# First attention of a Flamingo-style block on one core: the subtraction of the row maximum folded into the exp

## The reference

```
q = latents @ Wq                                   # 8 heads of 64
kv = concat([x, latents]) @ Wkv ; k, v = split(kv)
q = l2norm(q) * q_scale ; k = l2norm(k) * k_scale
sim = einsum('bhid,bhjd->bhij', q, k) * 8.0
sim = where(mask, sim, -max)
attn = softmax(sim)
out = layer_norm(einsum('bhij,bhjd->bhid', attn, v) @ Wo)
x = x + tanh(g) * out
```

## Time and profile before

| | us |
|---|---|
| median of 3 runs | 398.12 (397.4 to 398.33) |
| the profiled execution | 397.01 |
| its span in the trace | 394.9 |
| first attention, about | 24 to 192 of the span |
| experts, about | 192 to 260 |
| second attention and last part | 260 to 395 |

### The profile page before, as it was taken

How to read it: one execution, slowest core, us unless ns; L and a number is a source line. 1 busy time by engine, 2 the same in 40 slices (tenths; PEclk the granted TensorE clock), 3 DMA queues, 4 the chain that set the end, 5 groups by cost and what they waited for, 6 DMA issues and landing times. The chain is left out here.

```text
span 394.9 us, 10468 instructions
## 1 busy us (share of the span) xinstructions
PE 367.7 (93%) x3588; PEld 272.4 (69%) x3601; DVE 321.5 (81%) x916; ACT 262.1 (66%) x528; POOL 219.5 (56%) x380
## 2 busy tenths in 40 slices
PE   7799989999999999999999999999979999986785
PEld 6356656666676676667766788878867888765664
DVE  2989999899998998988746588756458899999796
ACT  2377767777777777776765222245658999887885
POOL 4655559666666667762604000007685887788653
PEclk9899999999999999999999999999999999999589
DMA  5989999900000000000000000000000000000003
GB/s 166 259 151 123 121 135 118 108 1 2 2 2 2 2 1 2 2 2 2 3 1 2 0 2 0 2 1 2 0 2 2 3 4 2 2 4 2 0 16 93
DMA packets 61034, 13.26 MB, mean 34 GB/s; under 512 B 51108, under 2 KB 60344, under 8 KB 60984
## 3 DMA queue, kind: packets, MB, share of 16 engines
q1 hardware_dynamic: 60196, 12.37, 22.9%
q10 hardware_dynamic: 660, 0.23, 0.2%
q0 software_dynamic: 128, 0.00, 0.0%
HBM read 11.55 MB, written 1.05 MB: 32 GB/s over the span
## 5 line engine op out<-in xcount | busy, mean ns | idle before, releaser
L407 POOL TENSOR_TENSOR a_rn<-a_ssq,neghalf 128x8 f32<-128x8 f32 x48 | 79.0, 1653 | 24.4 <-DVE a_ssq L1019 19.8
L90 POOL TENSOR_TENSOR nrow<-mrow 128x2 f32<-128x2 f32 x32 | 6.3, 196 | 56.8 <-DVE mrow L86 56.5
L1019 DVE TENSOR_REDUCE a_ssq<-q_home 128x8 f32<-128x512 f32 x48 | 32.2, 672 | 6.4 <-ACT q_home L798 6.2
L501 PE MATMUL a_x<-wkv_a,a_kvT 128*128 128x512 f32 x64 | 35.5, 637 | 1.2 <-ACT a_kvT L791 1.0
L804 ACT ACTIVATE kv_home<-a_x,maskcol 128x512 f32<-128x512 f32 x32 | 21.9, 684 | 19.9 <-PE a_x L501 19.9
L423 POOL TENSOR_TENSOR a_yr<-a_ymv,eps_row 128x1 f32<-128x1 f32 x16 | 3.0, 189 | 37.8 <-DVE a_ymv L1062 37.8
L1038 DVE TENSOR_REDUCE a_mx<-a_s 128x4 f32<-128x512 f32 x32 | 21.9, 686 | 2.0 <-PE a_s L527 1.9
L1950 DVE TENSOR_REDUCE b_mx<-b_s 128x16 f32<-128x1024 f32 x16 | 19.5, 1218 | 4.3 <-PE b_s L1548 4.0
L515 PEld LDWEIGHTS a_m<-ident,q_home 128*128 128x128 f32 x128 | 15.8, 143 | 9.7 <-issue 9.0
L816 ACT ACTIVATE kv_home<-a_m,cols 128x512 f32<-128x512 f32 x32 | 21.9, 685 | 0.6 <-PE a_m L515 0.4
L546 PE MATMUL a_m<-kv_home,p_home 128*64 128x65 f32 x512 | 22.0, 228 | 0.3 <-ACT p_home L826 0.3
(11 more groups left out here) (301 smaller groups left out, 1144.6 us busy)
## 6 DMA issues: line engine op xcount, KB each, us to landing
w_gu<-in_L_ffn_Wg_dram SPq DMA_DIRECT2D x4, 512.0 KB, 9.7
w_gu<-in_L_ffn_Wu_dram SPq DMA_DIRECT2D x4, 512.0 KB, 11.9
w_d<-in_L_ffn_Wd_dram SPq DMA_DIRECT2D x8, 256.0 KB, 8.0
out_dram<-xs SPq DMA_DIRECT2D x8, 128.0 KB, 1.8
xs<-in_x_dram SPq DMA_DIRECT2D x1, 640.0 KB, 7.6
cs<-in_ctx_dram SPq DMA_DIRECT2D x1, 640.0 KB, 9.1
wkv_a<-in_L_xattn_Wkv_dram SPq DMA_DIRECT2D x2, 256.0 KB, 6.6
nat<-in_L_ffn_w_dram SPq DMA_DIRECT2D x2, 256.0 KB, 3.2
```

What stands on the lines that cost most here:

```text
L407: nc.gpsimd.tensor_tensor(rn[:, tp, i, :], ssq[:, tp, i, :], neghalf[:, 0:H0], ALU.pow)\
L501: nc.tensor.matmul(p_x[:], kvT[:, tp, b * 2 * S:(b + 1) * 2 * S], wkv_a[:, INNER:2 * INNER], start=True, stop=True).then_inc(vproj_done, 1)
L1019: nc.vector.tensor_reduce(ssq[:, tp, i, :], sq[:, i, :].rearrange("p (h d) -> p h d", h=H0), AX.X, ALU.add).then_inc(reduced, 1)
```

## The change

The keys' scale becomes -8 instead of 8, so the banks hold negated scores. VectorE reduces each bank with a minimum (`row_least`, into `mn`), which is the negated maximum. ScalarE computes exp(-1 * negated score + mn), head by head, straight from the bank: four ACTIVATEs of 128 columns with `mn`'s column as bias, since a bias is one value per row and each head has its own. The subtraction and its semaphores `maxed` and `shifted` are gone. TensorE's `scores(t)` waits for the exps of tile t-1 (`exped`), and the first shared gate too. `row_least(s-2, 1)` stands where `shift(s-2, 0)` stood in VectorE's list.

```diff
--- before.py
+++ after.py
@@ -247,7 +247,7 @@
         kvT = sb("kvT", [P, 2, 4 * S])
         ssq = sb("ssq", [P, 2, 3, H0])
         rn = sb("rn", [P, 2, 3, H0])
-        mx = sb("mx", [P, 2, HP])
+        mn = sb("mn", [P, 2, HP])
         rsum = sb("rsum", [P, 2, HP])
         yst = sb("yst", [P, 2, 6])
         ymv = sb("ymv", [P, 2, 2])
@@ -280,9 +280,9 @@
         norms_ready, xn_ready, xT_done, affined, kv_masked, proj_done, squared, reduced, normed, scaled = (
             sem(n) for n in ("norms_ready", "xn_ready", "xT_done", "affined", "kv_masked", "proj_done", "squared",
                              "reduced", "normed", "scaled"))
-        vproj_done, v_ready, weigh_ready, q_turned, k_turned, qT_ready, kT_ready, scored, maxed, shifted, exped = (
+        vproj_done, v_ready, weigh_ready, q_turned, k_turned, qT_ready, kT_ready, scored, least_ready, exped = (
             sem(n) for n in ("vproj_done", "v_ready", "weigh_ready", "q_turned", "k_turned", "qT_ready", "kT_ready",
-                             "scored", "maxed", "shifted", "exped"))
+                             "scored", "least_ready", "exped"))
         pT_done, prT_ready, mixed, inverted, att_ready, attT_done, attT_ready = (
             sem(n) for n in ("pT_done", "prT_ready", "mixed", "inverted", "att_ready", "attT_done", "attT_ready"))
         y_done, y_stats, y_rstd, y_read, xb_ready, x_new, root_ready = (
@@ -520,7 +520,7 @@
                 pe.wait_ge(kT_ready, 2 * t + 2)
                 if t == 0:
                     pe.wait_ge(maskcol_ready, 1)
-                wait(pe, shifted, 2 * t)
+                wait(pe, exped, 2 * t)
                 for h in range(HP):
                     for a, b in ((0, 0), (1, 1), (0, 1), (1, 0)):
                         half = slice(a * DH0, (a + 1) * DH0)
@@ -601,7 +601,7 @@
 
             def shared_gate(i):
                 if i == 0:
-                    pe.wait_ge(shifted, 2 * NT)
+                    pe.wait_ge(exped, 2 * NT)
                 if i == 1:
                     pe.wait_ge(weights_out, 3)
                     pe.wait_ge(xrT_ready, 2)
@@ -817,8 +817,13 @@
                                      scale=cols[:, 4:5]).then_inc(kT_ready, 1)
 
             def exp(t, a):
-                act.wait_ge(shifted, 2 * t + a + 1)
-                nc.scalar.activation(pr[:, a], pr[:, a], ACT.Exp).then_inc(exped, 1)
+
+                act.wait_ge(least_ready, 2 * t + a + 1)
+                wait(act, pT_done, 2 * (t - 1) + a + 1)
+                for h in range(HP):
+                    last = nc.scalar.activation(pr[:, a, h, :], p_s[a][:, h * P:(h + 1) * P], ACT.Exp,
+                                                bias=mn[:, a, h:h + 1], scale=-1.0)
+                last.then_inc(exped, 1)
 
             def probs_out(t, a):
                 act.wait_ge(pT_done, 2 * t + a + 1)
@@ -989,7 +994,7 @@
                     last = nc.vector.tensor_copy(maskcol[b * S:(b + 1) * S, b:B:2], p_s0[b * S:(b + 1) * S, b:B:2])
                 last.then_inc(maskcol_ready, 1)
                 dve.wait_ge(scale_in, 16 * 4)
-                nc.vector.scalar_tensor_tensor(cols[:, 4:5], cols[:, 8:9], 8.0, cols[:, 9:10], ALU.mult, ALU.mult)\
+                nc.vector.scalar_tensor_tensor(cols[:, 4:5], cols[:, 8:9], -8.0, cols[:, 9:10], ALU.mult, ALU.mult)\
                     .then_inc(scale_ready, 1)
 
             def gate_rows():
@@ -1033,17 +1038,11 @@
                                                proj_bank[i][:].rearrange("p (h d) -> p h d", h=H0),
                                                ALU.min, ALU.mult).then_inc(scaled, 1)
 
-            def row_max(t, a):
+            def row_least(t, a):
+
                 dve.wait_ge(scored, t + 1)
-                nc.vector.tensor_reduce(mx[:, a, :], p_s[a][:].rearrange("p (h k) -> p h k", h=HP), AX.X, ALU.max)\
-                    .then_inc(maxed, 1)
-
-            def shift(t, a):
-                s3 = p_s[a][:].rearrange("p (h k) -> p h k", h=HP)
-                dve.wait_ge(maxed, 2 * t + a + 1)
-                wait(dve, pT_done, 2 * (t - 1) + a + 1)
-                nc.vector.tensor_tensor(pr[:, a], s3, mx[:, a, :].unsqueeze(2).to_broadcast([P, HP, P]),
-                                        ALU.subtract).then_inc(shifted, 1)
+                nc.vector.tensor_reduce(mn[:, a, :], p_s[a][:].rearrange("p (h k) -> p h k", h=HP), AX.X, ALU.min)\
+                    .then_inc(least_ready, 1)
 
             def attend(t, a):
                 dve.wait_ge(mixed, 2 * t + a + 1)
@@ -1158,25 +1157,21 @@
                 if exists(s - 1, NT):
                     scale(s - 1, (s - 1) % 2, 0)
                 if exists(s - 2, NT):
-                    row_max(s - 2, 0)
+                    row_least(s - 2, 0)
                 if exists(s - 1, NT):
                     reduce(s - 1, (s - 1) % 2, 2)
                     scale(s - 1, (s - 1) % 2, 1)
                 if exists(s - 2, NT):
-                    shift(s - 2, 0)
+                    row_least(s - 2, 1)
                 if exists(s - 3, NT):
                     attend(s - 3, 0)
                     attend(s - 3, 1)
                 if exists(s, NT):
                     replace_masked(s, s % 2)
-                if exists(s - 2, NT):
-                    row_max(s - 2, 1)
                 if exists(s - 1, NT):
                     scale(s - 1, (s - 1) % 2, 2)
                 if exists(s - 7, NT):
                     next_input(s - 7)
-                if exists(s - 2, NT):
-                    shift(s - 2, 1)
                 if exists(s - 5, NT):
                     row_stats(dve, s - 5, (s - 5) % 2, x_new)
                 if exists(s - 4, NT):
```

## The result

The changed kernel takes **403.46 us** (median of 4 runs, 403.17 to 403.5) against 397.76 for the kernel before beside it (median of 4, 397.07 to 398.33): ratio 1.014, 95% interval 1.0122 to 1.0157, so 4.9 to 6.2 us slower. Its profiled execution took 403.5 us with a span of 401.7, 6.8 more than the span before. The forecast was 405.1 in a range of 402.0 to 409.0.

A forecast was written before the change was run, and what follows sets the result against it. TensorE was taken to bound the steady turn of 10.79 us, with VectorE having slack. Terms 7.8 + 1.1 + 0.5 - 2.4 = +7.0 us on a profiled 397.0 gave 404.0, or 405.1 against the median of 398.1; range 402.0 to 409.0.

The forecast's parts named there:

- The loop: Steady turn: scores, TensorE's list through the keys' projection, Square, exp, scores; each turn 0.56 us longer.
- E: Time from the first exp piece's start to the last one's end in a bank, forecast 1.15 us.
- two-pointer rival: Each exp piece costs what the affine ACTIVATE costs, E 1.52: +12.9, 411.0 us; chance 0.06.
- short pieces: Exp pieces as short as plain copies, E 0.75: +0.6, 398.7 us; chance 0.05.
- tiles 1 to 14: Scores of these tiles each wait for the exp of bank 1: 14 x 0.56 = +7.8 us.
- given back in those turns: TensorE's waits for VectorE in turns 3 to 5 go as the subtractions are dropped: -2.4 us.
- tile 15: Turn without projections, where the exp starts later against the scores: +1.1 us.
- behind it, to the first shared gate: Last exp: tile 15's second-bank transposes and the tail wait for the longer exp, +0.5 us.
- VectorE as hidden pace-setter: Short hidden TensorE waits for VectorE in steady turns vanish: 396.1 us with 0.6 a turn; chance 0.05.
- ScalarE spilling over: Each exp's growth of 0.53 also reaches TensorE another way once per turn: 7.4 more, 412.5 us; chance 0.04.

The follow-up runs named there:

- no maximum: The kernel with both exps early, with the row minimum left out and one exp of 512 per bank: 395.04 us, 0.9943 of the kernel before.
- split-and-wait kernel: Kernel before, with each exp cut into four of 128 in SBUF and the scores waiting for the exps: 408.46 us, 1.0278 of before.
- both exps early: Changed kernel with bank 0's exp moved ahead of the first values on ScalarE and bank 1's right behind them: 394.33 us, 0.9916 of the kernel before.
- the split alone: Kernel before, with each exp of 512 cut into four of 128 in SBUF, the scores still waiting for the subtraction: 398.91 us, 1.0045 of before.
- one exp: Changed kernel with one exp of 512 columns per bank, using the first head's bias for all heads: 399.03 us, 0.9992 of the kernel before.
- changed again: The changed kernel run once more without any edit, on the same chip as its variants: 406.64 us, 1.0224 of the kernel before.

## Why the prediction was right

**The loop.** The step on which it all rested was that the exp starts behind the Square, and the Square behind TensorE's projection, so a turn is a fixed part plus E. Four values of E where the scores wait for the exp give 10.86 at 0.62, 10.92 at 0.68, 11.38 at 1.14 and 11.50 at 1.26: each is E + 10.24. The prediction's fixed part was 11.35 - 1.15 = 10.20. Most of the rest is the release: 0.14 from the exp's end to the scores' start, where 0.11 was taken from the key copy (181.88 to 181.98 in the earlier trace rows is 0.10).

**E.** Forecast 1.15 (pieces of 0.37, 0.26 apart), measured 1.13 to 1.15 with pieces of 0.373. By the Trainium skill's figures (ScalarE: Activation LUTs, What ACT_TABLE_LOAD costs) E was an estimated 1.27; the trace of the changed kernel stays below that, and the pieces out of SBUF, at 0.39 and 1.26 for four, come to the page's figures. The two-pointer rival (1.52) and the short pieces (0.75) both fall.

**The terms.** All from the starts of the scores in the two traces.

| term | forecast | measured |
|---|---|---|
| tiles 1 to 14 | 14 x 0.56 = 7.8 | 14 x 0.59 = 8.3 |
| given back in those turns | -2.4 | 5.26 - 8.3 = -3.0 |
| tile 15 | 1.1 | 9.58 - 8.50 = 1.08 |
| behind it, to the first shared gate | 0.5 | 11.72 - 11.33 = 0.39 |
| sum | 7.0 | 6.73 |

The 5.26 is tile 0's scores to tile 14's, 155.82 us after and 150.56 before. Only this sum is measured in the changed kernel; its split into 8.3 and -3.0 rests on the kernel with no maximum, where neither the new wait nor VectorE's waits are left: there the stretch is 147.61, which is 2.95 under before, and with 14 x 0.59 it comes to 155.87. So both terms were forecast too small, by 0.5 and 0.6, and that the sum is off by only 0.3 is in part luck: the two errors cancel. The rows of after that answer to the earlier trace rows:

```profile
187.19 1.14 ACT L824 ACTIVATE p_home<-a_s,a_mn 128x128 f32<-128x128 f32 x4
...
193.66 1.15 ACT L824 ACTIVATE p_home<-a_s,a_mn 128x128 f32<-128x128 f32 x4
```

```profile
188.47 1.10 PE L527 MATMUL a_s<-kv_home,q_home 64*64 64x128 f32 x32 [1.52 <-ACT p_home L824]
...
194.86 0.66 PE L537 MATMUL a_m<-ident,p_home 128*128 128x128 f32 x4 [0.41 <-ACT p_home L824]
```

**What VectorE gives back.** The waits of the earlier trace rows are gone in the profile after: the turns 4 and 5, 11.06 and 12.78 before, are 11.38 like the rest. The prediction named two reasons, a VectorE with less to do and a TensorE that arrives later. The runs show that they do not add. The split-and-wait kernel, which keeps the subtractions, pays 7.9 where 14 x 0.71 = 9.9 would stand (158.45 from tile 0's scores to tile 14's), so it gets 2 of the 3 us back by its late TensorE alone. The kernels that pay no wait get 2.7 (both exps early) and 2.95 (no maximum) back by the relief, up to tile 14's scores. Both exps early gains another 0.2 in the tail, where the last exp comes earlier; that makes its 2.9. The forecast of 2.4 was low mostly because it counted nothing for turn 4 (11.06 before, 0.27 over the steady 10.79) and for one later turn of 10.91 (0.12).

**Rivals.** VectorE as hidden pace-setter falls: no version has a steady turn under 10.79, not even the one that takes some 2 us a turn off VectorE (10.05 to 8.00 in the same turn). ScalarE spilling over falls for the changed kernel, whose turn is the loop's E + 10.24 with nothing on top, and holds at a small size in the split alone. The prediction looked for it in a late probability copy or affine, and took VectorE's 1 us to spare for room. It came by the Square, VectorE's sum behind it and the read of the output bank; a busy share of 93% (10.05 of 10.79) did not show how close that read lies to the next writer.

**The whole.** The medians differ by 5.7 us, the two profiled executions by 6.5 and their spans by 6.8. The forecast of 7.0 was made against a profiled execution of 397.0 and then laid on a median of 398.1; it sits 1.6 above the measured 403.46. 1.1 of that is that layer, since the profiled execution of before lay 1.1 under its first median and that of after (403.5) at its own. The other 0.5 is the forecast of 7.0 against the 6.5 of the profiled executions; 0.3 of it is the sum.

## What to carry to other kernels

When a reader of a PSUM bank is replaced by another engine, ask where in that engine's list the new reader stands: the bank's release moves to its end, and the price is how late that is for the next writer, not how busy the engines are. Here the same instructions made the first attention 6.7 us longer in one place of ScalarE's list and 2.9 shorter in another. Look for the idle time in the new reader's list (1.14 us a turn stood ahead of the values), and move the reader there together with the change.

## What the runs showed of the hardware

Four ACTIVATEs of 128 columns out of PSUM with a bias column take 1.13 to 1.15 us (0.373 each), out of SBUF 1.26 (0.39 each); one of 512 out of PSUM with it takes 0.68. Release from ScalarE to a waiting TensorE took 0.14 to 0.15 us (121.85 to 121.99 in the changed kernel, 122.56 to 122.71 with split and wait).

The experts' stage, whose work is the same in all these kernels, took 68.74 or 68.75 us in six of the ten profiles, at a granted clock of 1.00, and 72.09 or 72.10 in four (one exp, split and wait, changed again, no maximum), at a mean of 0.95. The changed kernel has one profile of each kind. The stage in the slower one:

```profile
198.66:270.76 72.10, 71.16 (x371) 53.55 (x369) 46.29 (x129) 26.75 (x47) 7.07 (x11) 0.95 0.00 1
...
198.66:206.00 7.34, 7.34 (x46) 5.37 (x45) 3.34 (x13) 4.61 (x9) 2.81 (x7) 0.96 0.00 0
206.00:209.00 3.00, 3.00 (x10) 2.15 (x10) 0.58 (x2) 1.11 (x2) 0.00 (x0) 0.50 0.00 0
209.00:212.00 3.00, 3.00 (x6) 1.27 (x5) 1.94 (x6) 1.90 (x3) 0.00 (x0) 0.50 0.00 0
```

From 206 to 212 us the clock is at its lower level (0.50, 1.2 GHz), with TensorE recorded busy without a gap in that stretch and in the 7.34 us before it. The last idle time recorded ahead of the fall is 0.15 us, at 194.76, and in the profile that stayed at 1.00 the same instructions have the same distance there (0.84 from one start to the next). So the granted clock went down with no recorded idle time of TensorE close before it, in some executions of a kernel and not in others. What decides it is open; no run here was made for it. It is why differences of a few us were read from the first attention's length, where the clock was 1.00.
